# One first stage instead of four in a graph attention and mixture-of-experts kernel

## The reference

```python
xn  = layernorm(x)                                # rows of 512
seq = (xn @ W_seq).reshape(2048, 16, 32)
s1, s2 = seq . a1, seq . a2                       # per node and head
scores = leaky_relu(s1[i] + s2[j], 0.2) + (1 - adj[i, j]) * -65500
hidden = softmax(scores) @ seq ; x = x + elu(hidden @ W_out + b_out)
x = x + top-2 gated experts(layernorm(x))         # 8 experts, 384
A = (adj + adj.T) / 2 + I ; d = rowsum(A) ** -0.5 # adj is 0/1, 0.8% ones
x = x + adj @ ((d * A * d) @ layernorm(x))
x = x + top-2 capacity experts(layernorm(x))      # 8 experts, 2048
```

## Time and profile before

| what | us |
|---|---|
| median of 3 runs | 2327.65 (2326.54 to 2328.87) |
| the profiled execution | 2330.49 |
| its span | 2328.7 |
| PE busy in the span | 1987.6 (85%) |
| DVE, ACT, POOL busy | 1286.3, 1053.9, 488.1 |
| mean granted clock of PE | 0.939 of full |

### The profile page before, as it was taken

The page is one execution under the profiler, slowest core; times in us unless marked ns, Lnnn a source line. Parts: engine busy times, 40 slices in busy tenths (PEclk is TensorE's granted clock), DMA queues, the critical chain, the costliest instruction groups (busy, mean ns, idle before and its releaser), DMA issues. The chain is left out here.

```text
span 2328.7 us, 39446 instructions
## 1 busy us (share of the span) xinstructions
PE 1987.6 (85%) x16165; PEld 1741.8 (75%) x16165; DVE 1286.3 (55%) x1627; ACT 1053.9 (45%) x1050; POOL 488.1 (21%) x338
## 2 busy tenths in 40 slices
PE   4594999999987609999946889845999999999998
PEld 4584999999986309999944778624888888888887
DVE  2556899999847616777759412253343343343342
ACT  4217899888802305555512013124353453453441
POOL 3271332222202050000036420047011010010111
PEclk9996999999998859999977999977999999999999
DMA  7607411111302066677746532046353443452433
GB/s 272 261 0 279 167 39 38 38 39 39 25 13 84 1 243 220 240 250 251 260 169 217 157 107 69 31 153 151 118 144 97 123 131 95 127 148 90 131 77 127
DMA packets 143087, 303.94 MB, mean 131 GB/s; under 512 B 15868, under 2 KB 39548, under 8 KB 138801
## 3 DMA queue, kind: packets, MB, share of 16 engines
q1 hardware_dynamic: 128704, 270.07, 34.7%
q0 software_dynamic: 14272, 32.28, 5.3%
HBM read 236.10 MB, written 74.91 MB: 134 GB/s over the span
## 5 line engine op out<-in xcount | busy, mean ns | idle before, releaser
L694 PE MATMUL attn_acc<-attn_vals,attn_mask 128*128 128x198 bf16 (+1 forms) x4096 | 474.4, 229 | 35.2 <-DVE attn_mask L635 26.0
L694 PEld LDWEIGHTS attn_acc<-attn_vals,attn_mask 128*128 128x128 fp8e4 x4096 | 393.0, 98 | 37.1 <-issue 33.7
L593 ACT ACTIVATE attn_mask<-attn_s_row,gat_big_s 128x2048 fp8e4<-128x2048 f32 x208 | 395.0, 1988 | 57.0 <-PE attn_acc L696 43.1
L696 PE MATMUL attn_acc<-attn_vals,gat_adj 128*128 128x99 bf16 x2048 | 283.4, 208 | 0.0
L1693 DVE TENSOR_TENSOR moe_w_lo<-moe_raw,moe_w_hi 128x2048 fp32r<-128x2048 f32 x64 | 146.8, 2293 | 234.1 <-ACT moe_w_hi L1650 234.1
L1650 ACT CAST moe_w_hi<-moe_raw 128x2048 fp32r<-128x2048 f32 x64 | 122.1, 1908 | 222.5 <-PE moe_y_ps L1618 191.7
L696 PE MATMUL attn_acc<-attn_vals,attn_below 128*128 128x99 bf16 x2048 | 202.2, 210 | 0.0
L323 PE MATMUL moe_h_ps<-moe_x_hi,moe_w_hi 128*128 128x512 f32 x512 | 200.0, 391 | 1.6 <-DVE moe_x_lo L1698 1.6
L324 PE MATMUL moe_h_ps<-moe_x_lo,moe_w_hi 128*128 128x512 f32 x512 | 199.7, 390 | 0.0
L325 PE MATMUL moe_h_ps<-moe_x_hi,moe_w_lo 128*128 128x512 f32 x512 | 199.7, 390 | 0.0
L696 PEld LDWEIGHTS attn_acc<-attn_vals,gat_adj 128*128 128x128 fp8e4 x2048 | 196.3, 96 | 0.0
(11 more groups left out here) (286 smaller groups left out, 4383.1 us busy)
## 6 DMA issues: line engine op xcount, KB each, us to landing
moe_raw<-in_L_ffn_W_dram SPq DMA_DIRECT2D x64, 1024.0 KB, 5.1
moe_wg<-in_L_ffn_w_gate_dram SPq DMA_DIRECT2D x23, 768.0 KB, 6.0
moe_wu<-in_L_ffn_w_up_dram SPq DMA_DIRECT2D x23, 768.0 KB, 7.7
moe_wd<-in_L_ffn_w_down_dram SPq DMA_DIRECT2D x23, 768.0 KB, 9.1
adj_a<-in_adj_dram SPq DMA_DIRECT2D x16, 1024.0 KB, 4.9
attn_s_row<-s_rows SPq DMA_DIRECT2D x16, 1024.0 KB, 4.8
sym_a<-in_adj_dram SPq DMA_DIRECT2D x32, 512.0 KB, 4.7
sent<-all_zeros SPq DMA_DIRECT2D x1, 11776.0 KB
```

The lines of the kernel that those rows point to most:

```text
L593: act.activation(mask[u][:, j, :], s1_row[:, u, :], ACT.Sigmoid, bias=big_s2[:, j, h:h + 1], scale=BIG, saturate=False).then_inc(stepped, 1)
L694: mm = pe.matmul(o[:, 0:first], mask[u][:, j, cols], both[:, 0:first], start=(j == 0 and b % 2 == 0), stop=(j == NT - 1), skip_group_check ...
L696: mm = pe.matmul(o[:, 3 * C1:6 * C1], second, both[:, 3 * C1:6 * C1], start=False, stop=(j == NT - 1), skip_group_check=True)
```

## The change

```diff
+                load_x(0)
+                load_a(0)
+                load_a(1)
+                load_x(1)
+                load_a(2)
+                load_x(2)
+                load_a(3)
+                load_x(3)
+                for t in range(4, NT):
+                    load_a(t)
...
                 for u in range(2):
+                    sp.wait_ge(cast, NT - 2 + u)
+                    sp.dma_start(s1_row[:, u, :], s1_rows[u:u + 1, :].to_broadcast([P, N])).then_inc(rows_in[u], 16)
+                sp.wait_ge(evacuated, 2 * NT)
                 for q in range(4):
+                    sp.dma_start(adjT_dram[512 * q:512 * q + 512, :].rearrange("(t p) n -> p t n", p=P),
+                                 raw[:, 4 * q:4 * q + 4, :]).then_inc(spilled[q], 16)
...
+                def evacuate(t):
+                    for f in range(2):
+                        dve.wait_ge(turned, 2 * t + f + 1)
+                        dve.tensor_copy(raw[:, 8 * f:8 * f + 8, t * P:(t + 1) * P], turned_ps[f][:],
+                                        saturate=False).then_inc(evacuated, 1)
+
+                def fill(q):
+                    dve.wait_ge(iso_kept, q + 1)
+                    dve.wait_ge(evacuated, 8 * q + 8)
+                    words = slice(q * P, (q + 1) * P)
+                    dve.tensor_tensor(adj8[:].bitcast(I32)[:, :, words], raw[:].bitcast(I32)[:, :, words],
+                                      iso8.bitcast(I32)[:, words].rearrange("p (a n) -> p a n", a=1).to_broadcast([P, NT, P]),
+                                      ALU.bitwise_or).then_inc(adj_done, 1)
...
+                    if what == "P":
+                        if i + 1 < NT:
+                            low_part(i + 1)
+                        if i % 4 == 0 and i + 4 < NT:
+                            variances(i // 4 + 1)
+                        if i % 4 == 1 and i + 3 < NT:
+                            scales(i // 4 + 1)
+                        if i + 2 < NT:
+                            norm(i + 2)
...
-    COMPARED = (7, 11, 15)
+    COMPARED = [(2, 5, 7, 10, 13, 15)] + [(7, 11, 15)] * (H - 1)
...
+        elif h == 1:
+            eng.wait_ge(spilled[j // 4], 16)
...
-                    eng.tensor_tensor(s[j % R][:], a[:, j % R, :], at[:, j % R, :], ALU.add).then_inc(built, 1)
+                    eng.tensor_tensor(s[j % R][:], a[:, j % R, :], at[:, j % R, :], ALU.subtract).then_inc(built, 1)
                 else:
-                    eng.copy(s[j % R][:], at[:, j % R, :]).then_inc(built, 1)
+                    eng.activation(s[j % R][:], at[:, j % R, :], ACT.Copy, scale=-1.0).then_inc(built, 1)
```

More of the change, by code:

```diff
@@ L191, in _ @@
                 act.activation(root[:], var[:], ACT.Sqrt).then_inc(root_ready, 1)
[L194 to L310, removed]
-                    terms = [(hi[u][:, j, :], lo[u][:, j, :], w_hi[:, j, :], w_lo[:, j, :]) for j in range(KD)]
-                    three_pass(pe, out[u][:], [(a, b, x[:, 0:D], y[:, 0:D]) for a, b, x, y in terms])
-                    three_pass(pe, sc[u][:], [(a, b, x[:, D:WC], y[:, D:WC]) for a, b, x, y in terms]).then_inc(summed, 1)
-                turn(0, 0)
-                rounds(pe, NT, 2, step)
@@ L326, in three_pass, with front_order, put @@
     return mm
-def transpose_adj(nc, k, adj, adjT, isolated, rowsum, colsum, x, x_sb, bn, W_seq, a1, a2, w, w_hi, w_lo):
-    with ExitStack() as st:
-        c = Ctx(nc, st, "adj")
-        a = c.sb("a", [P, 2, N])
-        ab = c.sb("ab", [P, 2, N], BF16)
-        turned_ps = [c.ps(f"turned{u}", [P, NT, P], BF16) for u in range(2)]
-        col_ps = c.ps("col_ps", [P, NT])
-        loaded = [c.sem(f"loaded{u}") for u in range(2)]
-        a_rows = c.sb("a_rows", [P, 2, DH])
-        prod = c.sb("prod", [P, KD, H, DH])
-        x_in = [c.sem(f"x_in{q}") for q in range(4)]
-        cast, turned, kept, ended, stats = (c.sem(x) for x in ("cast", "turned", "kept", "ended", "stats"))
-        w_in, halved, w_full, w_high, w_split = (c.sem(x) for x in ("w_in", "halved", "w_full", "w_high", "w_split"))
-        passed = c.sem("passed")
+def front_order():
+    order, held = [("A", 0), ("A", 1)], []
+    def put(item, then=()):
+        order.append(item)
+        order.extend(held)
+        held[:] = then
+    for p in range(NT):
+        put(("P", p), [("T", p // 4)] if p % 4 == 3 else [])
+    for n in range(2, NT):
+        put(("A", n), [("M", n - 2)] if n < 4 else [("I", n // 4)] if n % 4 == 3 else [])
+        if n == 4:
+            order.append(("I", 0))
+    return order + held
@@ L407, in _ @@
[L407 to L414 removed]
+                ch = Chain(dve, ch_v)
@@ new lines, in project @@
+                def project(p):
+                    if p + 1 < NT:
+                        turn(p + 1)
+                    pe.wait_ge(low, p + 1)
+                    for f in range(2):
+                        if p:
+                            pe.wait_ge(copied, 2 * p + f - 1)
+                            pe.wait_ge(scored, 2 * p + f - 1)
+                        three_pass(pe, out[f][:], [(hi[p % 2][:, j, :], lo[p % 2][:, j, :], w_hi[:, j, f, :], w_lo[:, j, f, :])
+                                                   for j in range(KD)]).then_inc(summed, 1)
@@ L630, in masks @@
[L630 to L642 removed]
+                        dve.wait_ge(rows_in[h % 2], 16 * (h // 2 + 1))
@@ L1455, in _ @@
             def _(act):
+                if gather is not None:
+                    act.wait_ge(deg_ready, 1)
+                    act.activation(root[:], deg[:], ACT.Sqrt).then_inc(deg_rooted, 1)
+                    act.wait_ge(dinv_ready, 1)
                 for j in range(NT):
```

554 lines of the change are left out of this document (359 added, 195 removed).

## The result

| | before | after |
|---|---|---|
| median, us | 2328.26 (2326.54 to 2331.9, 4 runs) | 2286.85 (2286.12 to 2291.09, 4 runs) |
| profiled execution, its span | 2330.49, 2328.7 | 2291.09, 2289.1 |
| mean granted clock | 0.939 | 0.931 |

The ratio is 0.9824, 95% interval 0.9807 to 0.9841: 1.8% or 41 us faster, where 39.5 us were forecast.

A forecast was written before the change was run, and what follows sets the result against it. One serial chain of stages ending on TensorE was taken as the bound; first stages -40.4, attention +1.5, graph products -0.6 sum to -39.5 us, giving 2288 us from a median of 2327.65, range 2278 to 2298.

The forecast's parts named there:

- P0 at 32: Start of the first projection on PE, after loads, statistics and w_lo: 32 us, bounds 29.5 and 35.
- Projections 66, last one ends at 98: Sixteen projections: 56 us of PE work plus slow start, transposes and stalls make 66, bounds 60 and 75.
- rival 5: Projections stay at 1.2 GHz: 56 us more, 2344 us in all; chance 0.02.
- Fourteen tiles and tail 52: Adjacency tiles after the projections: 48 us bound by DVE, copies at 1.22 us, plus a tail of 4.
- Rival 1: Adjacency evacuation copies fast (0.69 us), ACT and loads bound the tiles: 2281 us; chance 0.12.
- rival 4: Evacuation into strided 8-bit rows slower: above 2.6 us per copy takes all the gain, 4 us gives 2365; chance 0.04.
- t0 at 150: Start of the attention block (first Sigmoid table load): at 150 us against 190.4, 40.4 us earlier.
- Rival 3: One ordered list for all engines idles PE 0.7 us in each of 30 items: t0 at 167, 2305 us; chance 0.13.
- The row of head 2 at t0+66: Head 2's s1 row, queued behind spills and zeros, lands 66 us after attention starts; head 0's 10 us are given back.
- rival 2: Head 2's row does not hold attention back, head 0's 10 us gain stays: 2277 us; chance 0.08.
- Head 2's end 1.5 later against t0: Attention: head 2 ends 1.5 us later relative to the attention's start than before; range -10 to +5.
- Graph products -0.6: Graph products after attention: 8-bit adjT halves 256 KB loads beside the first gathers, 0.6 us less.

The follow-up runs named there:

- experiment 4: Changed kernel with DVE normalizing tile i+2 ahead of the variances and ACT taking the root one tile later: 2288.07 us, ratio 0.9809 to the kernel before.
- Experiment 5: Changed kernel with each DVE evacuation copying 512 instead of 1024 elements, the rest a constant from POOL (measurement only): 2291.32 us, ratio 0.9822 to the kernel before.
- experiment 7: The changed kernel again, unedited, as a control: 2290.87 us, ratio 0.9829 to the kernel before.
- Experiment 1: Changed kernel with the 20.4 MB of zeros in 14 pieces behind the s1 rows of heads from 2 on: 2269.29 us, ratio 0.9732 to the kernel before.
- Experiment 8: Changed kernel with the token tags sent in eight pieces of 512 rows behind the s1 rows of heads 3 to 10: 2284.91 us, ratio 0.9809.
- 3: Changed kernel with zeros in pieces behind the s1 rows, head 0's masks made as before (three compared, applied by fours): 2275.27 us, ratio 0.9763.

## Why the prediction was right, step by step

- *P0 at 32*: the first 272-column matmul is at 33.6, since the small rows came at 12.2, not 10, and DVE's w_lo ended at 32.8 instead of 30.9; PE stood 2.4 us for it. A miss of 1.6. POOL's a2 half ended at 25.9, not at 20.8 to 22, but ahead of w_lo.
- *Projections 66, last one ends at 98*: 61.4, ends at 95.0. From 66.19 to 68.07 us a matmul of 272 columns starts every 0.125 us (0.127 forecast), so rival 5 falls. The granted clock reads 1.00 throughout, but from 34.01 to 36.27 they start every 0.226, at half the later pace: some 1.0 of the 3 us forecast for the start was paid. The variances' stalls were put at 6; experiment 4 gets 4.2 back.
- *Fourteen tiles and tail 52*: 51.2. The copies took 1.22 us, the value worked out from the earlier trace rows. The Trainium skill (VectorE: DVE Perf Modes, What auto-detection actually checks) gives single speed for a copy from PSUM with an 8-bit output, and the trace agrees: 1217 ns for 1024 elements. Rival 1 falls by this row, and rival 4 (a copy of 2.6 us or more). PE sat at the 1.2 GHz level here (0.56 of full over the stretch), which the prediction hadn't foreseen; it was not the bound, since DVE was busy 92% of the stretch. Experiment 5 shows by its 3.7 us how near the next limits are.
- *t0 at 150*: 146.2, and 145.1 in experiment 7. Rival 3 (coupling, t0 = 167) falls: at DVE, the bound, the one order for all engines cost some 2 us of idle time, not 0.7 in each item.
- *PE at t0+4.7, head 0's end at t0+45, head 1's at t0+74*: t0+4.2, +45.5, +75.
- *The row of head 2 at t0+66*: t0+66.2. PE's gap is 14.6 us (13 forecast). That is the step on which the forecast stood: it turned 10 us of gain in head 0 into none. Experiment 1 shows it, and rival 2 falls.
- *Head 2's end 1.5 later against t0*: this term was mis-sized. It was +4.1 (t0+121.7 against t0+117.6). The row is 1.7 of it (t0+66.2 against t0+64.5), as forecast; the other 2.4 come behind the row. The prediction let head 2 end 18 us after DVE's last flip (the row plus 35), as it does before. In the run PE waited for no flip once it had started at 235.5. It started late, because DVE came to the combine 21.3 us after the row, not 18: its two operations ahead of that took 3.93 and 3.85 us instead of 2.29 while POOL computed values. And it started slowly: in the gap and until 241 the granted clock is 0.50 (37 matmuls in the 15 us from 225), and head 2 then takes 32.0 us instead of 29.45. The upper bound of +5 had named the clock as its reason.
- *Nothing behind head 2*: wrong by 5. Head 13 takes 35.1 us instead of 29.45, 4.1 of it the stall by issue, where before it was 31.2 with 1.6: 3.9 us. The prediction had no term for TensorE's instruction stream. Experiment 8 shows the transfer that made it here. The other full heads take 29.45 us where before they took 29.35, in all of the changed kernel's variants: 1.2 us over twelve, of a cause that no run looks for.
- *Graph products -0.6*: not shown either way. The symmetric product is 3.0 shorter here, but 147 to 149 us in the changed kernel's variants and 150 before; PE's wait for z_lo in it is 58.3 us after and 60.8 before, but 59.8 in experiment 7 and 61.1 in experiment 8.

The sum, -39.5 against -39.6 between the profiled executions, is thus closer than its terms: t0 was 3.8 better, the attention 7.7 worse, the rest 4.0 better than forecast. That they cancel to 0.1 is luck, and the last of them lies within the spread of single executions. What was right is the mechanism: the first stages shrink by some 40 us, and the row of head 2 takes back what head 0 gains.

## What to carry to other kernels

Ask of each stage that is shortened what the next one's loads stand behind: one early, large, unhurried transfer in the same queue as a small hurried one made the small one the clock of the attention: with it the change brought 39.6 us of span, and 52.3 when neither kernel had it (62.0 from the kernel before to experiment 1, but 9.7 of these the zeros cost the kernel before too). Cut such a transfer in pieces and put each behind the load that is urgent. An edit's worth in a stage can be read from the length of that stage, where the time of the whole still hides it: the projections (61.4 us) and the tiles with the tail (51.2) repeated within 0.1 us in after and experiments 1, 3, 7 and 8, while t0 itself moved from 145.1 to 146.3 with the start of P0.

## What the runs showed of the hardware

- A transfer of 4096 rows of 8 bytes (32 KB) kept the DMA queues over 90% busy for some 7 us at 1 to 48 GB/s, and a stall of TensorE of 4 us, with no semaphore behind it, began 1 us after that (567.05). Whether it comes depends on more than the transfer: whole at 538 us it caused none, in pieces among the pieces of zeros there were 3.8 us of stalls, in pieces alone none. Instruction loads of 16 KB, in a queue of their own, share the 16 engines: one came 12.6 us after the one before it instead of 7.3 and took 3.9 us instead of 1.0, and landed inside the stall, 2.7 us before its end. That it is the cause is likely and wasn't tested by itself.
- An int32 DVE operation over 128x2048 bytes, 2.29 us alone, took 3.93 and 3.85 while POOL's tensor_tensor over 128x1056 ran, and 3.0 to 4.1 beside it elsewhere in the attention; four 8-bit copies from PSUM that ran wholly beside POOL took 1214 to 1225 ns, as the others did (1201 to 1225).
- ACT copies 128x1024 from PSUM to 8-bit in 1015 ns, DVE in 1217.
- 20.4 MB of zeros and 4.2 of spills in one queue put the 1 MB row behind them 66.2 us behind t0: 70.1 us from the first spill (142.31) for 25.6 MB, 2.7 us per MB.
